# Attention inside a three-layer block on one core: the products of probabilities and v of a unit as one set of four matmuls over 512 queries instead of two sets over 256

## The reference, cut to what matters

```python
def _msa(x, w_qkv, w_proj):                     # B, N, D, H, DK of the shape used: 8, 512, 128, 16, 8
    qkv = (x @ w_qkv).reshape(b, n, 3, H, DK)
    q, k, v = ...
    attn = jnp.einsum('bhnd,bhmd->bhnm', q, k) * (1.0 / np.sqrt(DK))
    attn = jax.nn.softmax(attn, axis=-1)
    y = jnp.einsum('bhnm,bhmd->bhnd', attn, v)
    return y.transpose(0, 2, 1, 3).reshape(b, n, d) @ w_proj
```

## Time and profile before

| what | value |
|---|---|
| timed runs | 1472.48, 1475.89, 1477.49 us (median 1475.89) |
| the profiled execution, its own time | 1473.18 us |
| its span in the profile | 1471.4 us |
| mean granted TensorE clock | 0.909 of full speed |
| busy share PE / DVE / ACT / POOL | 84% / 71% / 58% / 38% |
| first mixer phase, exponents and pv | 61.8 to 462.8 us of the span |
| second mixer phase, the same | 931.9 to 1332 us of the span |

### The profile page before, as it was taken

One profiled execution on the slowest core, in us unless ns is written; L12 is line 12 of the kernel. 1 busy time (PEld: TensorE's weight loads), 2 busy tenths in 40 slices (PEclk: granted clock), 3 DMA queues, 4 the chain that ended last, 5 costly groups with the idle time before them and its releaser, 6 DMA issues. The chain is left out here.

```text
span 1471.4 us, 36051 instructions
## 1 busy us (share of the span) xinstructions
PE 1230.9 (84%) x12512; PEld 661.3 (45%) x12513; DVE 1042.9 (71%) x1842; ACT 860.7 (58%) x1742; POOL 553.6 (38%) x797
## 2 busy tenths in 40 slices
PE   2799999999997596398888754999999999993893
PEld 1234444444443596145455442344444444442893
DVE  3889988988992332478788745888898988963232
ACT  2288877778775353444334411588788778881451
POOL 6122324323212354355676536222332431222462
PEclk9599999999999799599999955799999999996896
DMA  4322442222110121100000003122122122100224
GB/s 117 71 74 74 130 121 68 82 71 73 55 36 9 53 67 47 42 2 3 3 2 2 3 1 87 57 75 65 49 82 73 53 81 66 56 15 30 56 66 122
DMA packets 81540, 82.40 MB, mean 56 GB/s; under 512 B 16249, under 2 KB 53724, under 8 KB 81392
## 3 DMA queue, kind: packets, MB, share of 16 engines
q1 hardware_dynamic: 72560, 69.88, 16.7%
q0 software_dynamic: 4608, 8.44, 1.8%
q10 hardware_dynamic: 4224, 2.10, 0.5%
HBM read 50.42 MB, written 29.93 MB: 55 GB/s over the span
## 5 line engine op out<-in xcount | busy, mean ns | idle before, releaser
L986 DVE TENSOR_REDUCE maxima<-ps 128x2 f32<-128x1024 f32 x512 | 616.2, 1222 | 89.8 <-PE ps L652 88.5
L933 ACT ACTIVATE probs<-ps 128x512 f32<-128x512 f32 x1024 | 550.8, 600 | 120.3 <-PE ps L660 109.7
L652 PE MATMUL ps<-k_stack,q_stack 62*128 62x512 f32 x1024 | 390.0, 473 | 39.0 <-DVE maxima L986 21.7
L660 PE MATMUL ps<-q_stack,k_stack 64*128 64x512 f32 x1024 | 396.3, 464 | 4.2 <-ACT q_whole L869 3.4
L670 PE MATMUL ps<-probs,v_stack 128*32 128x256 f32 x4096 | 329.6, 394 | 0.9 <-ACT probs L933 0.4
L652 PEld LDWEIGHTS ps<-k_stack,q_stack 62*128 62x128 f32 x1024 | 160.1, 194 | 235.9 <-issue 138.3
L660 PEld LDWEIGHTS ps<-q_stack,k_stack 64*128 64x128 f32 x1024 | 159.2, 187 | 30.5 <-ACT q_whole L869 8.6
L670 PEld LDWEIGHTS ps<-probs,v_stack 128*32 128x32 f32 x4096 | 81.7, 108 | 166.6 <-issue 148.3
L532 POOL CAST neg_wide<-maxima 128x16 fp32r<-128x16 f32 x64 | 12.6, 196 | 286.7 <-DVE maxima L986 286.7
L1299 POOL DMA_INDIRECT expert_out<-yt,number x80 | 78.3, 979 | 72.4 <-POOL number L1295 44.1
L1276 DVE COPY w_now<-w 128x512 f32 x80 | 34.6, 433 | 80.1 <-issue 42.2
(11 more groups left out here) (208 smaller groups left out, 1622.7 us busy)
## 6 DMA issues: line engine op xcount, KB each, us to landing
q_stack<-q_split SPq DMA_DIRECT2D x256, 64.0 KB
k_stack<-k_split SPq DMA_DIRECT2D x512, 32.0 KB
q_split<-q_parts SPq DMA_DIRECT2D x16, 512.0 KB, 2.7
k_split<-k_parts SPq DMA_DIRECT2D x16, 512.0 KB, 3.6
xt<-sorted SPq DMA_DIRECT2D x80, 64.5 KB
w<-in_L_ffn_w SPq DMA_DIRECT2D x16, 256.0 KB, 3.0
rows<-expert_out SPq DMA_DIRECT2D x16, 256.0 KB, 4.5
x_all<-in_L_attn_x SPq DMA_DIRECT2D x8, 256.0 KB, 5.1
```

Source lines behind the costliest of these rows:

```text
L652: mm = t.matmul(psS[:, h, :], qs[g][score_rows(h), h // 2, u * P:(u + 1) * P], ks[g][score_rows(h), h // 2, :], start=True, stop=True)
L660: t.matmul(ring("e", G, u, n), ks[G % NG][half(h), h // 2, u * P:(u + 1) * P], qs[G % NG][half(h), h // 2, :], start=True, stop=True).then ...
L933: a.activation(probs[u % 2][:, h, :], ring("e", G, u, n), ACT.Exp, scale=float(DK) ** -0.5).then_inc(e_read, 1)
L986: v.tensor_reduce(maxima[G % 2][:, :, pair, u:u + 1], psS[:, 2 * pair:2 * pair + 2, :], AX_X, ALU.max, negate=True).then_inc(s_read, 1)
```

## The change

`pv` loses its argument `part`. For a unit it is now called once, behind exponent 3, and issues four matmuls over all 512 queries in place of two sets of four over 256. The scores and exponents of a unit stand one behind the other in front of it. The waits on `v_staged` and `o_kept` stand ahead of it, the wait on `e_read` is the same. The special place at u = 1 is gone.

```diff
-                def pv(unit, part):
+                def pv(unit):
 
                     g, u = unit // TPB % NG, unit % TPB
-                    if part == 0:
-                        pe.wait_ge(e_read, 4 * unit + 4)
-                    here = slice(part * T // 2, (part + 1) * T // 2)
+                    pe.wait_ge(e_read, 4 * unit + 4)
                     for h in range(GROUP):
-                        last = t.matmul(psO[VW * h:VW * (h + 1), here], vs[g][:, u, h, :], probs[u % 2][:, h, here],
-                                        start=(g % SHARE == 0 and u == 0 and part == 0),
-                                        stop=(g % SHARE == SHARE - 1 and u == TPB - 1 and part == 1))
-                    if part:
-                        last.then_inc(pv_unit, 1)
+                        last = t.matmul(psO[VW * h:VW * (h + 1), :], vs[g][:, u, h, :], probs[u % 2][:, h, :],
+                                        start=(g % SHARE == 0 and u == 0),
+                                        stop=(g % SHARE == SHARE - 1 and u == TPB - 1))
+                    last.then_inc(pv_unit, 1)
...
-                        if ahead:
-                            score(G + 2, u, 0)
-                        exponent(G, u, 0)
-                        if ahead:
-                            score(G + 2, u, 1)
-                        exponent(G, u, 1)
-                        if u != 1:
-                            values(0)
-                        if ahead:
-                            score(G + 2, u, 2)
-                        exponent(G, u, 2)
+                        for n in range(GROUP):
+                            if ahead:
+                                score(G + 2, u, n)
+                            exponent(G, u, n)
                         if u == 1:
-                            values(0)
-                        if ahead:
-                            score(G + 2, u, 3)
-                        exponent(G, u, 3)
-                        values(1)
+                            pe.wait_ge(v_staged, G + 1)
+                            if g % SHARE == 0 and G:
+                                pe.wait_ge(o_kept, shared(b, g))
+                        if unit:
+                            pv(unit - 1)
                         for kind, j in jobs(b, g, u):
                             job(kind, j)
 
-                for part in range(2):
-                    pv(TPB * NG * B - 1, part)
+                pv(TPB * NG * B - 1)
```

More of the change, by code:

```diff
@@ L796, in _ @@
                         unit = TPB * G + u
[L798 to L804, removed]
-                        if ahead:
-                            score(G + 2, u, 0)
-                        exponent(G, u, 0)
-                        if ahead:
-                            score(G + 2, u, 1)
-                        exponent(G, u, 1)
-                        if u != 1:
-                            values(0)
-                        if ahead:
-                            score(G + 2, u, 2)
-                        exponent(G, u, 2)
-                        if u == 1:
-                            values(0)
-                        if ahead:
-                            score(G + 2, u, 3)
-                        exponent(G, u, 3)
-                        values(1)
+                        for n in range(GROUP):
+                            if ahead:
+                                score(G + 2, u, n)
+                            exponent(G, u, n)
+                        if u == 1:
+                            pe.wait_ge(v_staged, G + 1)
[3 more added lines that the diff above has]
+                            pv(unit - 1)
                         for kind, j in jobs(b, g, u):
                             job(kind, j)
-                for part in range(2):
-                    pv(TPB * NG * B - 1, part)
+                pv(TPB * NG * B - 1)
                 for kind, j in AFTER:
```

## The result

| | before | changed |
|---|---|---|
| timed runs, median | 1474.74 us (1472.48 to 1477.49) | 1501.51 us (1500.18 to 1503.42) |
| ratio | | 1.0182, 95% interval 1.0159 to 1.0204 |
| span of the profiled execution | 1471.4 us | 1498.3 us |
| one full sequence (16 units) | 52.36 us | 54.37 us |

The change costs 26.8 us. All of it lies in the two mixer phases: from the first pv set to the transposes of the last finished sum the first one takes 415.8 us (61.70 to 477.46) where it took 402.2 (61.80 to 463.97), the second 413.7 (944.8 to 1358.49) where it took 400.7 (931.9 to 1332.56), 13.6 and 13.0 us more.

The account below looks back on a forecast made before the run. PE was taken as the first bound, DVE 11% behind; after the change exponent 3's wait would bind. 31 us for units with scores plus 6 without gave 37 us, stated as 1512 us for the median, range 1484 to 1540.

Parts of the forecast that it names:

- Part 1: In pv on PE: one joined set takes 1.00 us against 1.14 for two halves, a gain of 0.14 us.
- The last rival: Exponent 3 waits for its bank and the joined set wins nothing (1.14 us): 2.76 per unit, 1549 us; chance 0.06.
- Part 2: Eight score and exponent matmuls in a row on PE cost 1.15 us against 1.34, gaining another 0.19.
- Part 3: Exponent 3 waits for ACT to empty exponent 0's bank, holding back pv: plain unit 2.62 us against 2.48, 0.14 slower.
- Part 4: Units with a side job: (2,1) takes 3.63 us against 3.34; a sequence some 54.4 us, 0.13 more per unit.
- Part 5: Score-bank loop between PE and DVE: 4.92 us for two units, 2.46 each, below 2.62, so it costs nothing.
- The first rival: Exponent 3's wait does not bind, PE's shorter work counts: 0.31 us less per unit, 1397 us; chance 0.11.
- The rival in which gain and loss cancel: Plain unit stays at 2.48 us; only 16 units without scores lose, some 0.25 each: 1480 us; chance 0.06.
- The sum: Over both phases: 240 units with scores x 0.13 = 31 us, 16 without x 0.37 = 6 us: 37 us slower.
- The 0.37 us of a unit without scores: Units without scores, 8 in each phase: 2.24 us now, 2.61 new, 0.37 more, 16 times.

## Why the prediction was right, point by point

The direction and the mechanism were right, and the time, 1501.5 us, lies within 1484 to 1540. The forecast of 1512 was 10 us too high: 37 us were counted and 26.8 measured. (By its own terms the sum gives 1513, which is 2.5% above 1476.)

- **Part 1, the joined set**: 1.00 us forecast from the earlier trace rows, 1.00 measured (257.39 to 258.39). The last rival, that joining would win nothing, falls.
- **Part 2, eight in a row**: with no wait they would have ended at 1.15 us; the fourth score starts 0.82 us into the unit, where the fourth pair was put for the case without a wait. Only the fourth exponent didn't follow.
- **Part 3, the ring**: exponential at 0.55, exponent 3 at 1.20, pv at 1.63, unit 2.62 forecast; 0.54, 1.19, 1.62, 2.62 measured. The runs with shortened exponentials show that this chain is the cause.
- **Part 4, side jobs**: for (2,1) 3.63 us forecast, 3.64 measured (244.60 to 248.24); for a whole full sequence 54.4 forecast and 54.37 measured.
- **Part 5, the score pairs**: not reached in the changed kernel, as said. With exponential 0 halved the chain of part 3 gives 0.54 + 0.44 + 0.43 + 1.00 = 2.41, just under the 2.46 of the loop. The unit (3,2) took 2.40: DVE had stood idle for 0.54 us ahead of its reductions there and had slack. In the second phase, where DVE reduces back to back, PE waits for it ahead of the second pair in two units one behind the other, and the two take 4.90 us (929.94 to 934.84) where 4.92 were counted:

```profile
928.36 4.71 DVE L968 TENSOR_REDUCE maxima<-ps 128x2 f32<-128x1024 f32 x4 [1.14 <-PE ps L652]
929.94 0.49 PE L652 MATMUL ps<-k_stack,q_stack 62*128 62x512 f32 x1
...
930.77 0.18 PEld L652 LDWEIGHTS ps<-k_stack,q_stack 62*128 62x128 f32 x1 [0.53 <-DVE maxima L968]
...
933.12 0.18 PEld L652 LDWEIGHTS ps<-k_stack,q_stack 62*128 62x128 f32 x1 [0.40 <-DVE maxima L968]
...
934.84 0.50 PE L652 MATMUL ps<-k_stack,q_stack 62*128 62x512 f32 x1
```

- **The first rival** (PE's shorter work counts, 1397 us) falls. The Trainium skill's page "TensorEngine Tiling (Array Packing)", section Tiling Modes, says that changing the tiling mode drains TensorE; the run with two halves one behind the other agrees (1.00 us for both, 1.14 with a change of mode after each). The drains saved stand in front of a wait and buy nothing. The rival in which gain and loss cancel (1480 us) falls too: the lone exponent holds pv back by 0.43 us, not by 0.33.
- **The sum is the step that was mis-sized**: "240 units with scores x 0.13 = 31 us". Each phase can be parted at the starts of `turn_h`, and the loss of each stretch read from the two timelines:

| stretch | units | counted per phase | first phase | second phase |
|---|---|---|---|---|
| first pv set to the first `turn_h` | 28 | 3.6 | 0.6 | 1.2 |
| the four full sequences | 64 | 8.3 | 8.2 | 8.2 |
| the next 16 units | 16 | 2.1 | 0.6 | 0.6 |
| the next 16, five of them without scores | 16 | 3.3 | 1.6 | 1.6 |
| from there to the last transposes | 3 | 1.1 | 2.5 | 1.4 |
| sum | 127 | 18.4 | 13.6 | 13.0 |

It holds in the full sequences. Behind them there are fewer side jobs on PE, because no slice is left to prepare, and 3.2 us are missing in each phase. DVE's side work is the later one in some units there: from `rank` to `turn_y` it took 5.69 us before and 5.67 after, and DVE reduced back to back in both. The timeline of DVE in the changed kernel:

```profile
1269.95 0.43 DVE L1066 CAST slot<-slot_f 128x4 int32<-128x4 f32 x1
1270.30 4.60 DVE L967 TENSOR_REDUCE maxima<-ps 128x2 f32<-128x1024 f32 x4
```

and in the kernel before, in the same two units:

```profile
1247.42 0.43 DVE L1085 CAST slot<-slot_f 128x4 int32<-128x4 f32 x1
1247.77 4.61 DVE L986 TENSOR_REDUCE maxima<-ps 128x2 f32<-128x1024 f32 x4
```

I took the loss of one steady sequence for all of them, without a look at how the cover changes where side jobs are missing. How much of the 3.2 us is DVE's doing no run shows. The 0.37 us of a unit without scores came out in four of the seven from (2,0) to (3,2) (0.36 to 0.44, from one exponent 0 to the next); the other three went from 0.1 less to 0.2 more.

- **The clock at both ends of a phase** took another part, which the sum leaves out. In the profile of before the units of the first phase ran at 1.2 GHz until about 69 us, in that of after until about 65, with PE busy without a break in both; from the first pv set to the `m` job of the sixth unit it took 15.7 us before (61.80 to 77.50) and 13.0 after (61.70 to 74.74), although the later units are longer. In the second phase the 1.2 GHz lasted until about 937 before, 5 us behind the first pv set (931.91), and until about 946 after, 1 us behind it (944.80). Halving the eight us or so of difference gives an estimate of 4 us in favour of the changed kernel, most of the 5.5 us that the first row of the table lacks. It is not shown that the change does this: with the old order and exponential 0 halved the clock also rose by about 64 us, and with the set in the middle and the later place at u = 1 only at about 66. At the ends it went the other way. In the changed kernel the clock fell to 1.2 GHz at about 471 us, ahead of the last two sets, although PE had been busy for 3.55 of the 4 us from 466 to 470. The run with exponential 1 halved has the same order on PE, and its clock stayed at 2.4 GHz to the end. From the last `turn_h` to `gate` both take 6.03 us; then they part. First the changed kernel, then that run, each with a window (stretch, length, busy times, granted clock as a share of 2.4 GHz) and PE's timeline:

```profile
472.00:477.50 5.50, 4.78 (x23) 0.94 (x23) 0.97 (x6) 2.01 (x4) 0.00 (x0) 0.50 0.00 0
472.71 1.93 PE L668 MATMUL ps<-probs,v_stack 128*32 128x512 f32 x8
...
477.46 0.90 PE L682 MATMUL ps<-ident,oT 128*128 128x128 f32 x3 [0.72 <-ACT oT L826]
```

```profile
470.00:476.00 6.00, 4.94 (x38) 2.11 (x35) 1.91 (x11) 2.56 (x6) 0.00 (x0) 1.00 0.01 3
472.93 1.06 PE L668 MATMUL ps<-probs,v_stack 128*32 128x512 f32 x8
...
475.92 0.66 PE L682 MATMUL ps<-ident,oT 128*128 128x128 f32 x4 [0.72 <-ACT oT L826]
```

The last row's stretch takes 11.63 us in both phases of that run, 13.67 and 12.57 in the changed kernel and 11.13 and 11.15 before. So some 3 of the 26.8 us are the clock at the phases' ends in this one profile, and not the ring.

## What to carry to other kernels

Before instructions are grouped to save changes of kind on an engine, count how many buffers the group fills: with three banks, a block of four outputs waits for the consumer's whole latency (here 0.55 us to the start of the first exponential and 0.60 for it), and everything behind it in an in-order queue waits too. What stood between was not only a cost but also the cover of that latency. Group where something else already breaks the block, here a side job, and leave the split where nothing does; and price a change over the stretches in which other engines are late as well as over the steady one.

## What was not expected of the hardware

- Two sets of four float32 matmuls over 256 columns and one set over 512 take the same 1.00 us when they stand directly behind each other; no price for the number of instructions can be seen here, only one for the change of kind (0.14 us a set, 0.57 against 0.43).
- The time at which the clock rises at the start of a mixer phase differed by some 4 us between profiled executions, also between kernels with the same order of instructions: at about 69 us in the profile of before and at about 64 us in the same order with exponential 0 halved. From the first pv set to the first `turn_h` the first took 87.43 us and the second 84.70; in the second phase, where both clocks rose about 5 us behind the first pv set, they took 86.07 and 85.75.
- The end of a phase differs in the same way: with one order of instructions on PE the clock fell at about 471 us in one profile and not before 476 in another, which made the same last stretch 13.67 or 11.63 us long.
